# One convolution step of a Mamba and feed-forward layer, placed elsewhere in VectorE's written order of work

## What is computed

```python
xz = einsum('bld,ed->ble', x, W_in);  xi, z = split(xz, 2)          # 512 inner channels each
xc = sum(xpad[:, k:k + L, :] * conv_w[:, k] for k in range(4))       # convolution over 4 tokens
u  = silu(xc + conv_b)
dbl = einsum('blc,ec->ble', u, W_xproj)                              # 16 for dt, 16 for B, 16 for C
dt = softplus(dbl[..., :16] @ W_dt.T + b_dt)
h  = h * exp(dt * A) + (dt * u) * B;  y = sum over 16 states of h * C   # token after token
y  = (y + u * D_skip) * silu(z);  x = layernorm(x + y @ W_out.T)
g, p = x @ w_gate.T, x @ w_up.T                                      # 768 hidden
x  = layernorm(x + (silu(g) * p) @ w_down.T)
```

## Time and profile before

| | |
|---|---|
| median of 3 runs | 1805.21 us (1802.66 to 1806.15) |
| the profiled execution | 1806.15 us, of which the instructions span 1804.4 us |
| TensorE (PE) busy | 1738.6 us, 96% of the span |
| ScalarE (ACT) busy | 1713.0 us, 95% |
| VectorE (DVE) busy | 1703.1 us, 94% |
| GpSimd (POOL) busy | 1494.9 us, 83% |
| mean granted clock of TensorE | 0.991 of full speed |
| steady chunk | about 108 us |

### The profile page before, as it was taken

The page is one execution under the profiler, slowest core; times in us unless marked ns, Lnnn a source line. Parts: engine busy times, 40 slices in busy tenths (PEclk is TensorE's granted clock), DMA queues, the critical chain, the costliest instruction groups (busy, mean ns, idle before and its releaser), DMA issues.

```text
span 1804.4 us, 40427 instructions
## 1 busy us (share of the span) xinstructions
PE 1738.6 (96%) x15678; PEld 1213.7 (67%) x15678; DVE 1703.1 (94%) x2003; ACT 1713.0 (95%) x2907; POOL 1494.9 (83%) x852
## 2 busy tenths in 40 slices
PE   7779999999999999999999999999999999999997
PEld 3456676767667676676767767676676767667676
DVE  5989999999999999999999999999999999999974
ACT  6899999999999999999999999999999999999971
POOL 5887997979979797997979979797997979989850
PEclk9899999999999999999999999999999999999999
DMA  7040120303013040221303013040221304012000
GB/s 210 1 120 1 10 112 15 118 1 97 36 15 118 14 118 1 31 102 15 118 2 105 28 15 118 15 118 1 46 87 15 118 1 119 15 37 84 1 25 24
DMA packets 171487, 100.57 MB, mean 56 GB/s; under 512 B 139408, under 2 KB 157584, under 8 KB 163232
## 3 DMA queue, kind: packets, MB, share of 16 engines
q1 hardware_dynamic: 171296, 97.98, 19.2%
HBM read 88.52 MB, written 9.44 MB: 54 GB/s over the span
## 4 chain that ended last, share of the span: by engine, by line
PE 45%; ACT 26%; DVE 15%; issue 9%; POOL 4%; DMA 0%; ACTq 0%; POOLq 0%; DVEq 0%
PE ring L1174 17%; PE tp L1153 13%; ACT decay L704 9%; DVE h L915 8%; ACT hT L711 7%; PE yb L1167 7%; PE ring L1266 4%; DVE acc L936 4%; POOL drive L568 3%; PE ring L1211 2%; ACT L741 2%; ACT acc L720 1%; PE ring L1232 1%; ACT sz L741 1%; ACT u L737 1%
## 5 line engine op out<-in xcount | busy, mean ns | idle before, releaser
L568 POOL TENSOR_TENSOR drive<-dtu,b_all 128x1024 f32<-128x1024 f32 x511 | 1215.5, 2413 | 7.9 <-DVE h L915 5.6
L704 ACT ACTIVATE decay<-dt,a_neg 128x512 f32<-128x512 f32 x1024 | 706.6, 718 | 9.4 <-DVE h L915 8.6
L1153 PEld LDWEIGHTS tp<-ident,h 128*128 128x128 f32 x4096 | 463.2, 141 | 245.8 <-issue 122.6
L915 DVE TENSOR_TENSOR_SCAN h<-decay,h,drive 128x512 f32<-128x512 f32 x512 | 620.6, 1268 | 7.5 <-ACT decay L704 2.6
L915 DVE TENSOR_TENSOR_SCAN h<-decay,drive 128x512 f32<-128x512 f32 x512 | 592.7, 1210 | 26.0 <-ACT decay L704 23.8
L711 ACT ACTIVATE hT<-tp 128x512 f32<-128x512 f32 x1024 | 595.9, 618 | 15.8 <-PE tp L1153 14.9
L1153 PE MATMUL tp<-ident,h 128*128 128x128 f32 x4096 | 564.0, 277 | 40.2 <-ACT hT L711 31.5
L1167 PE MATMUL yb<-hT,diag_c 128*32 128x128 f32 x8192 | 276.2, 277 | 6.4 <-ACT yt L732 5.3
L1167 PEld LDWEIGHTS yb<-hT,diag_c 128*32 128x32 f32 x8192 | 211.1, 110 | 82.2 <-issue 48.3
L1174 PE MATMUL ring<-xt,w_in 128*128 128x512 f32 x512 | 245.1, 602 | 2.4 <-ACT acc L752 2.4
L936 DVE SCALAR_TENSOR_TENSOR acc<-xi,cw,acc 128x512 f32<-128x512 f32 x189 | 160.3, 869 | 14.6 <-ACT xi L722 10.7
(11 more groups left out here) (134 smaller groups left out, 1673.5 us busy)
## 6 DMA issues: line engine op xcount, KB each, us to landing
b_all<-bc_scratch SPq DMA_DIRECT2D x63, 1024.0 KB, 7.3
xt<-in_xT SPq DMA_DIRECT2D x16, 512.0 KB, 4.6
res<-in_x SPq DMA_DIRECT2D x16, 512.0 KB, 6.2
out<-res SPq DMA_DIRECT2D x15, 512.0 KB, 2.9
c_col<-bc_scratch SPq DMA_DIRECT2D x256, 2.0 KB, 2.4
bc_scratch<-dbl SPq DMA_DIRECT2D x16, 64.0 KB, 1.6
b_all<-bc_scratch SPq DMA_DIRECT2D x2, 512.0 KB, 4.5
w_g<-in_w_gT SPq DMA_DIRECT2D x1, 768.0 KB, 7.3
```

The lines of the kernel that those rows point to most:

```text
L568: tt(drive[:, j % 4, :, :], src, b_all[:, n:n + 2, :], ALU.mult).then_inc(g_dr, 1)
L704: act(decay[decay_slot(k.parity, i)][:, :], dt[:, cb, :], ACT.Exp, scale=a_neg[:, cb, n:n + 1]).then_inc(a_da, 1)
L915: nc.vector.tensor_tensor_scan(h[:, h_slot(k.parity, q), at:at + T, i % 4], decay[decay_slot(k.parity, i)][:, :], drive[:, (i // 2) % 4, i ...
L1153: last = nc.tensor.transpose(tp[g % 2][:, b * P:(b + 1) * P], h[:, h_slot(k.parity, q), t0:t0 + TS, :].rearrange("p t s -> p (t s)"), iden ...
```

## The change

The first step of the convolution of the chunk to come, ("conv", 0, 0), is taken out of hook (3, 3), where it stood alone in front of r1 0, and put into the list of hook (5, 3), behind max 1 and norm 0 and in front of the other eleven steps. Nothing else is changed: not the instructions, nor their number, nor their semaphores, nor the tables of the other engines, nor the tables of the first and the last chunk.

```diff
 DVE_SIDE = {
-    (2, 1): [("skip", 3), ("clamp", 1)], (3, 3): [("conv", 0, 0), ("r1", 0)], (4, 2): [("r1", 1)],
-    (5, 3): [("max", 1), ("norm", 0), ("conv", 0, 1), ("conv", 1, 0), ("conv", 1, 1), ("conv", 2, 0), ("conv", 2, 1), ("conv", 3, 0), ("conv", 3, 1)],
+    (2, 1): [("skip", 3), ("clamp", 1)], (3, 3): [("r1", 0)], (4, 2): [("r1", 1)],
+    (5, 3): [("max", 1), ("norm", 0), ("conv", 0, 0), ("conv", 0, 1), ("conv", 1, 0), ("conv", 1, 1), ("conv", 2, 0), ("conv", 2, 1), ("conv", 3, 0), ("conv", 3, 1)],
```

## The result

The changed kernel takes 1810.01 us (median of 16 runs) and the kernel before 1805.19 us beside it (16 runs). The ratio is 1.0031, with a 95% interval of 1.0024 to 1.0038: it is slower by 0.3%, 4.8 us. The profiled execution took 1812.64 us, of which 1810.9 are the span, 6.5 more than the span before.

A forecast was written before the change was run, and what follows sets the result against it. Four engines nearly full, ScalarE with 0.8 us idle per chunk; 7 even chunks x 0.46, 6 odd x 0.45 and the first steady chunk's -0.9 give +5.0 us, so 1810.2 us; range 1802 to 1816.5.

The forecast's parts named there:

- The size: Whole kernel: +5.0 us on the median of 1805.21, so 1810.2 us, 0.28% slower.
- my repeating terms: Steady chunks after the first: each even one pays 0.46 us, each odd one 0.45 us.
- The lone step: VectorE at (3, 3): held up by GpSimd's drive, 1.9 to 2.0 us; moving it makes VectorE 1.2 us less busy per chunk.
- Where the saving goes: VectorE up to the list: only decay 19's wait is gained, 0.12 us (even), 0.30 (odd), 1.6 (first steady chunk).
- rival B: VectorE's 1.2 us set the pace: faster, about 1794 us, if the list's start moves over 0.75 us; chance 0.12.
- The step in the list: VectorE's list at (5, 3): twelve steps for eleven, 0.75 us more per chunk.
- ten of the eleven steps already stand so: In the list: these steps have the one they wait for directly in front, so nothing is added to 0.75 us.
- The slack: Behind the list: tanh 0 has 0.21 us (even), 0.10 (odd); up 1 has 0.17 (even), none (odd).
- The waits behind the list: Tanh 0 on ScalarE and up 1's weight load on TensorE show a new wait of 0.4 to 0.6 us.
- The pair of chunks: Two neighbouring steady chunks take 216.9 us for 216.0.

The follow-up runs named there:

- tiny_alone: Kernel before, with the lone step at (3, 3) on 1 column in place of 512 in chunks 2 to 15; 1802.57 us, ratio 0.9998.
- Tiny_in_list: Changed kernel, with the moved step in the list on 1 column in place of 512 in the steady chunks; 1803.01 us, ratio 0.9994 to the kernel before.
- twice_in_list: Kernel before, lone step left at (3, 3) and done a second time in the list at (5, 3); 1812.86 us, ratio 1.0048.
- before_r1: Kernel before, with the lone step moved from (3, 3) to hook (4, 2) ahead of r1 1; 1802.46 us, ratio 0.9994.
- u2_first_before: Kernel before, with u 2 put ahead of tanh 0 and tanh 1 in ScalarE's order at (6, 0); 1809.08 us, ratio 1.0027.
- hid_early: Changed kernel, with hid 0 on VectorE one scan earlier, hook (6, 1) for (6, 2); 1813.76 us, ratio 1.0049 to the kernel before.

## Why the prediction came true, step by step

- **The size.** 1810.2 us were forecast and 1810.01 measured; +5.0 against +4.8. This is nearer than the working deserves: the traces of the two profiled executions are 6.5 us apart in their spans, and the 13 periods, which the start does not disturb, 7.45 where my terms give 7 x 0.46 + 6 x 0.45 = 5.9. The first steady chunk gives 0.8 back; 7.45 - 0.8 = 6.65 fits the 6.5 of the spans. The rest of the way to 4.8 is scatter between executions: the profiled one stands 2.6 us above the median after and 1.0 before. So my repeating terms were 1.5 us too small, and that the total is right to 0.2 is luck.
- **The lone step: right.** It is held up by a drive on GpSimd; tiny_alone shows it with a step of one column. My reading that it ends 0.35 us behind the first drive took the middle of the pair for the end of that drive; the first ends at 699.29, 0.55 us before the step, and the second is the longer one because the step holds it up. VectorE is 12.3 us less busy, of 17 expected. The convolution steps alone are 16.4 less (160.3 to 143.9 in the lines view), so that term was right; a clamp (L944) takes 2.9 more, of which one instance of 3.5 us has the most, and the remainder I have not traced.
- **Where the saving goes: right.** It is waited away at r1 1 (1.18 us) and at scans 18 and 23. Only the gain at decay 19 is used, which is 0.61 us behind decay 18 everywhere, as forecast. In the first steady chunk, from decay 18 to the end of the list (scan 24), it was 183.33 - 160.37 = 22.96 us and is 182.34 - 160.19 = 22.15: -0.8 for -0.85 forecast. This also shows rival B wrong: the list started 0.1 to 0.3 us earlier against ScalarE's work, not 0.75.
- **The step in the list: a term mis-sized.** 0.75 forecast, 0.78 measured. What failed is "ten of the eleven steps already stand so". In fact seven of the eleven wait for the step directly in front of them. The moved step makes an eighth (tap 1 of block 0 now follows tap 2 at once), and a step that is waited for so costs 0.78 us, not the mean of 0.75. Tiny_in_list shows what hangs on a step beside its 512 columns, 0.25 us.
- **The slack: the step that failed.** In the odd chunk I read the 0.10 us between the end of heads and tanh 0 as slack (the sum did not use it, since it took 0 from up 1). In the changed kernel, where tanh 0 surely waits, it starts 616.96 - (616.67 + 0.20) = 0.09 us behind heads: the hand-over itself. So there was no slack in the odd chunk. In the even one tanh 0 had 0.21 - 0.09 = 0.12, less than the 0.17 that I subtracted for up 1, and the smaller slack decides. The slack also counts in the six even lists whose end lies inside the 13 periods, not in seven. From an odd list to an even one the terms are then 0.78 - 0.12 = 0.66 us, and 0.71 measured. From an even list to an odd one they are 0.78 - 0.12 - 0.30 = 0.36, and 0.41 measured. That is 7 x 0.66 + 6 x 0.36 = 6.8 us in 13 periods for 7.45. The missing 0.05 us in a period shows in twice_in_list too (0.82 for 0.78, 0.70 for 0.66), where nothing was removed. So it hangs on the added step; what it is stays open.
- **The waits behind the list: half right.** Tanh 0 waits, by 0.70 us (odd), beyond the 0.4 to 0.6 forecast, and 0.55 (even), within them. TensorE waits too, but for gs 0 ahead of up 0 (0.36 us), not for hid 0 ahead of up 1; once up 0 is late, up 1 follows it without idle time, and the waits of its weight loads for hid 0 grow only from 6.2 to 8.6 us in 14 places. I had looked at up 1 alone, because only there a load stood right behind its releaser. Up 0 starts 0.99 us behind the start of gs 0 before (odd chunk) and 0.74 after, when it waits; so it had 0.25 us of room, less than the shift (0.30 in the even chunk).
- **The pair of chunks:** 216.9 us forecast, 217.1 measured (108.91 + 108.17).

## What to carry to other kernels

A piece of work that is held up where it stands isn't cheap to move if the engine waits for others there anyway: count its saving only up to the next wait that another engine ends, and its cost from the place where it will stand. A long run of work without waits in it, with three engines waiting for its end, is the dearest place in such an order, and one step more in it costs its full length. Slack read as the distance between an end and a start must be lessened by the hand-over, here 0.09 us from GpSimd to ScalarE, and of several paths the smallest slack counts.

## What the runs showed that I had not expected

- The convolution step, a VectorE instruction with its two tensor inputs in SBUF, is held up beside a drive on GpSimd until that one has ended, whatever its own size. With one column it ends 0.01 to 0.02 us behind the drive (1.39 to 1.47 us long, 2.15 in the first steady chunk), with 512 columns 0.55 us behind it (1.90 to 2.01 us, 2.69 in the first steady chunk; 1.68 to 1.75 at the later place of before_r1, and 0.73 in its first steady chunk, where only 0.19 us of the drive are left). In the quiet list it costs 0.25 and 0.78. And it works the other way as well: the drive behind the full step takes 0.45 us longer.
- Putting one piece of 0.5 us ahead of two others on a full engine, with nothing added, costs 3.7 us in 13 periods (u2_first_before), half as much as the change itself; a scan that is 1.0 us later (hid_early) costs 2.2.
- The start of the program, the same in all these kernels up to the first steady chunk, differs by up to 5 us from one profiled execution to the next, at a granted clock of 0.92 to 0.95, so that a difference of a few us in one trace has to be read from the repeating stretch.
